# Transposes of the identity into an idle PSUM bank during the opening waits of a two-stream attention and expert kernel

## What is computed

```python
x = x + 0.5 * ffn(layernorm(x), ...)      # first half
x = x + attn(layernorm(x), ...)           # middle: grouped-query attention with rotary embedding
x = x + 0.5 * ffn(layernorm(x), ...)      # second half, same weights as the first
```

## Time and profile before

| What | Value |
|---|---|
| Median of 3 runs | 1806.88 us |
| Lowest, highest | 1806.15, 1808.86 us |
| The profiled execution | 1805.85 us |
| Its span, first to last instruction | 1803.9 us |
| TensorE matmuls busy | 1436.7 us (80%) |
| VectorE busy | 1197.7 us (66%) |
| ScalarE busy | 1095.6 us (61%) |
| GpSimd busy | 620.2 us (34%) |
| Mean granted TensorE clock | 0.913 of 2.4 GHz |

### The profile page before, as it was taken

The page is one execution under the profiler, slowest core; times in us unless marked ns, Lnnn a source line. Parts: engine busy times, 40 slices in busy tenths (PEclk is TensorE's granted clock), DMA queues, the critical chain, the costliest instruction groups (busy, mean ns, idle before and its releaser), DMA issues. The chain is left out here.

```text
span 1803.9 us, 34159 instructions
## 1 busy us (share of the span) xinstructions
PE 1436.7 (80%) x11800; PEld 640.8 (36%) x11801; DVE 1197.7 (66%) x1856; ACT 1095.6 (61%) x2032; POOL 620.2 (34%) x897
## 2 busy tenths in 40 slices
PE   2899999999508963799999999999999999607970
PEld 1333333433305541333333333333333433305540
DVE  5788888887202326588888888888888888112322
ACT  1578878878303321578888888887878887403320
POOL 1333343311261122646644433332333311261126
PEclk8799999999758985799999999999999999858995
DMA  6533444421011114333333333323333321011113
GB/s 207 128 91 104 106 112 118 126 64 31 1 47 46 47 33 101 73 87 102 86 95 77 84 99 90 85 71 94 81 96 81 94 50 31 1 45 45 44 32 92
DMA packets 85126, 139.57 MB, mean 77 GB/s; under 512 B 26736, under 2 KB 53104, under 8 KB 84976
## 3 DMA queue, kind: packets, MB, share of 16 engines
q1 hardware_dynamic: 57264, 83.24, 17.8%
q0 software_dynamic: 25664, 48.32, 10.8%
q10 hardware_dynamic: 2048, 6.03, 1.0%
HBM read 78.47 MB, written 56.10 MB: 75 GB/s over the span
## 5 line engine op out<-in xcount | busy, mean ns | idle before, releaser
L929 DVE TENSOR_REDUCE maxima<-banks 128x2 f32<-128x1024 f32 x768 | 925.0, 1223 | 174.1 <-PE banks L610 168.4
L906 ACT ACTIVATE work<-banks 128x512 f32<-128x512 f32 x1536 | 829.1, 598 | 121.6 <-PE banks L626 106.7
L610 PE MATMUL banks<-K,Q 64*128 64x512 f32 x1536 | 571.4, 461 | 67.4 <-DVE maxima L929 35.3
L626 PE MATMUL banks<-Q,K 64*128 64x512 f32 x1536 | 567.6, 451 | 9.1 <-ACT work L906 8.5
L638 PE MATMUL banks<-work,V 128*9 128x256 f32 x6144 | 476.6, 382 | 2.3 <-ACT work L906 0.8
L610 PEld LDWEIGHTS banks<-K,Q 64*128 64x128 f32 x1536 | 229.4, 189 | 225.4 <-DVE maxima L929 121.3
L626 PEld LDWEIGHTS banks<-Q,K 64*128 64x128 f32 x1536 | 229.1, 185 | 190.9 <-issue 140.8
L638 PEld LDWEIGHTS banks<-work,V 128*9 128x9 f32 x6144 | 91.5, 88 | 276.3 <-issue 205.8
L545 POOL TENSOR_TENSOR lo<-full,hi 128x512 fp32r<-128x512 f32 x44 | 56.2, 1277 | 312.6 <-ACT hi L813 214.0
L1295 ACT ACTIVATE work<-banks,ln 128x128 f32<-128x128 f32 x80 | 36.5, 457 | 187.1 <-PE banks L1244 187.1
L1319 DVE COPY work<-banks 128x512 f32<-128x512 f32 x80 | 55.3, 691 | 121.8 <-PE banks L1255 121.1
(11 more groups left out here) (153 smaller groups left out, 1373.6 us busy)
## 6 DMA issues: line engine op xcount, KB each, us to landing
Q<-q_scratch SPq DMA_DIRECT2D x188, 192.0 KB, 3.5
K<-k_scratch SPq DMA_DIRECT2D x376, 64.0 KB, 3.2
q_scratch<-hi POOLq DMA_DIRECT2D x44, 256.0 KB, 4.6
q_scratch<-lo POOLq DMA_DIRECT2D x44, 256.0 KB, 6.7
k_scratch<-hi POOLq DMA_DIRECT2D x22, 256.0 KB
k_scratch<-lo POOLq DMA_DIRECT2D x22, 256.0 KB
work<-sorted_x SPq DMA_DIRECT2D x80, 64.0 KB, 1.7
sorted_y<-work POOLq DMA_DIRECT2D x80, 64.0 KB, 1.8
```

Source lines behind the costliest of these rows:

```text
L610: fill(nc.tensor.matmul(bank, q4[parts(j), n % SLOTS, j // 2, qt * P:(qt + 1) * P], k4[parts(j), n % SLOTS, j // 2, :], start=True, stop=T ...
L626: nc.tensor.matmul(scp[x % EXPS][:, :], k4[parts(j), n % SLOTS, j // 2, kt * P:(kt + 1) * P], q4[parts(j), n % SLOTS, j // 2, :], start=Tr ...
L906: nc.scalar.activation(prob[:, kt, j ^ 1, :], scp[x % EXPS][:, :], ACT.Exp, scale=SCALE).then_inc(s.probs, 1)
L929: nc.vector.tensor_reduce(c.maxima[:, at:at + 9:8], c.banks[:, k * S:(k + 2) * S].rearrange("p (m n) -> p m n", m=2), AX.X, ALU.max).then_ ...
```

## The change

A list `WARM` gives three counts for each stream. A helper issues that many transposes of the identity matrix, with the identity as the other operand, into the first 128 columns of bank 4. None of them waits for a semaphore or signals one. They stand in three places of TensorE's program: before everything else of the stream (60 in stream 0, 90 in stream 1), before `loaded(0)` (100 and 150), and after the four matmuls of each query tile in the maxima of step 0 (10 each time, so 40 per stream). The tile's name in the trace is `banks<-ident`.

```diff
@@ -52,6 +52,7 @@
 AHEAD = 2
 SLOTS = 5
 EARLY = 2
+WARM = ((60, 100, 10), (90, 150, 10))
@@ -737,6 +738,11 @@
                 for j in range(J):
                     max_score(n, qt, j)
 
+            def warm_up(n):
+
+                for _ in range(n):
+                    nc.tensor.transpose(scp[0][:, 0:P], c.ident[:, :], c.ident[:, :])
+
@@ -757,14 +763,17 @@
+            warm_up(WARM[label][0])
             if label == 0:
                 pe.wait_ge(c.weights, 16 * c.first_loads)
             for n in range(-8, -4):
                 group(n, 0)
                 group(n, 2)
+            warm_up(WARM[label][1])
             loaded(0)
             for qt in range(QT):
                 maxima(0, qt)
+                warm_up(WARM[label][2])
             turn_max(0)
             loaded(1)
```

## The result

The changed kernel took 1815.36 us in the median of six runs (1813.72 to 1818.68), the kernel before 1806.88 in its six. The ratio is 1.0049 with an interval of 1.0036 to 1.0062, about 9 us slower, and outside the range. The profiled execution took 1818.68, the slowest of the six; its span is 1816.8 against 1803.9. So its own 12.8 us are not the median's 9.

What follows compares the result with a forecast made beforehand. It held that waits bound the openings, with slow-clock TensorE work on stream 1's path, and VectorE the maxima of step 0. Gains of 2.25 and 1.84 us summed to 4.1, from 1806.88 to 1802.8 us; range 1796 to 1808.

Steps and rivals of the forecast that it cites:

- 90 in stream 1: Train at stream 1's start: 12.4 us, from 669.6 to 682.0, hidden by a wait until 682.2.
- All slow, 19.8: Upper bound for the 90 transposes at stream 1's start if all ran at 1.2 GHz, ending at 689.4.
- rival 3: Both streams: transposes do not hold the clock up, all take 0.22 us; 29 to 39 us slower; chance 0.12.
- Transposes count for the clock: All trains: transposes count as work for TensorE's clock, so it rises; based on one mixed stretch with four transposes.
- 60: Train at stream 0's start: 9.1 us, from 6.9 to 16.0, hidden by VectorE's norm.
- 100: Train before stream 0's load: 11 us, from 25.5 to about 36.6, covered by the DMA wait until 38.1.
- 150: Train before stream 1's load: 16.5 us, from 690.7 to 707.2, against a wait until 708.0.
- Stream 1, first part, 2.25 us: Stream 1's opening: transposes 0.5 us sooner, projections q and qs 1.75 less, carried through to 708.0.
- The maxima, 0.92 per stream: From the first maxima into step 1's: faster matmuls and transposes save 0.92 us, twice 1.84.
- The tens, "cost nothing": After each query tile: 1.1 us fast, hidden under VectorE's 2.28; if slow, 2.3 us per stream.
- Maxima of step 1 stay slow: Rest of step 1's maxima, both streams: clock expected to fall after the last ten transposes, so no gain.
- rival 1: Clock lasts through step 1's maxima: some 4 us more in stream 0, about 2 in stream 1; 1797; chance 0.18.

Runs made afterwards that it cites:

- e5_gathers_late: Changed kernel with all trains, eight of the twelve gathers moved behind batch 0's norm in stream 1; ratio 0.9998 to the kernel before.
- e4_wide: Changed kernel with stream 1's 90 transposes replaced by 12 matmuls of 512 columns; ratio 1.0002 to the kernel before.
- e9_best: Kernel before plus trains of 90, 120 and 10 in stream 1 only, with eight gathers late; ratio 0.9995 to the kernel before.
- e13_wide_late: Kernel before plus 12 and 15 wide matmuls in stream 1 only, with eight gathers late; ratio 0.9984 to the kernel before.
- e12_tens: Kernel before plus only the 10 transposes after each query tile, in both streams; ratio 1.0027 to the kernel before.
- e11_hundred: Kernel before plus only the 100 transposes before the load in stream 0; ratio 1.0003 to the kernel before.
- e7_sixty: Changed kernel with 60 transposes instead of 90 at the start of stream 1; ratio 1.0037 to the kernel before.
- e8_wide_s1: Kernel before plus wide matmuls in stream 1 only (12, 17, 1), gathers not moved; ratio 1.0005 to the kernel before.
- e2_only90: Kernel before plus only the 90 transposes at the start of stream 1; ratio 1.0034 to the kernel before.
- e14_wide_all_late: Kernel before plus wide matmuls (0, 15, 1 in stream 0; 12, 15, 0 in stream 1), eight gathers late; ratio 0.9976 to the kernel before.
- e6_wide_all: Changed kernel with all trains as wide matmuls (8, 13, 1 and 12, 17, 1), gathers not moved; ratio 0.9989 to the kernel before.

## Why the prediction was wrong, point by point

- **The step that failed** is "90 in stream 1: 5 + 67 x 0.11 = 12.4 us, from 669.6 to 682.0, against 682.2". The train took 20.4 us there, to 692.1, and 12.2 in e5_gathers_late, where eight gathers come later. The price was right for a train with four gathers beside it. What failed with it is the sentence "Nothing queues behind a new wait, since none is added, and no DMA is issued", which put the cost of the neighbours at nothing. I had looked at the stretch for what TensorE waits for, not for what else was at work: twelve indirect DMAs on GpSimd. I named only the wait until 682.2 as cover and priced nothing for the neighbours. "All slow, 19.8" was in the list of bounds, and nearly what happened, but I gave it the cause of a cold clock and the chance of rival 3. What did happen, a train that overshoots although the clock is up, had 0.02.
- **Transposes count for the clock**: right. It reads 0.50 beside transposes alone from 671.7 to 677.6 and 1.00 behind them. The Trainium skill, "TensorE: Matmul & The Clock Gate", Part 4: PE-mode transpose, holds that the full clock does not engage in transpose mode; these rows disagree, and the measurement decides. So rival 3 had the sign, by luck, and not the mechanism: its pace of 0.22 all through did not occur, nor its 29 to 39 us. The working of the slow step is circular as written (0.43 from 0.22 and 0.22 from 0.43); the steps measured, 0.21 to 0.22 slow and 0.11 fast, bear it out.
- **60**: forecast 9.1 us and an end at 16.0; measured 9.21 from 6.94, an end at 16.15. Right.
- **100**: forecast 11, to 36.6; measured 11.34, to 36.5. Right. The first maximum was 0.8 late all the same, which I had put at nothing.
- **150**: forecast 16.5, measured 16.57. Right in size, but the cover was as thin as I wrote: with the stall gone the first maximum began right at its end (e4_wide, e5_gathers_late), so the gain before it could not pass. 120 and 15 wide ones leave the room.
- **Stream 1, first part, 2.25 us**: right in size where nothing stalls. From the first transpose to SyncE's first write of Q it is 2.3 to 2.4 in all four kernels with trains and late gathers (9.33 against 6.95 to 7.02). Up to the first maximum it is 2.0 in e9_best and 2.4 in e13_wide_late; in e5_gathers_late 0.8 (23.75 against 24.54), for its 150 end last. In the changed kernel the stall swallowed it.
- **The maxima, 0.92 per stream**: right in stream 1 of the changed kernel, where the first maximum and the end of the transposes in the maxima of step 1 lie 13.27 us apart (716.92, 730.19) against 14.20 before (707.99, 722.19). In stream 0 the cold tens ate it: 14.67 (38.90, 53.57) against 14.19.
- **The tens, "cost nothing"**: nearly right in stream 1 of the changed kernel, where ten take 1.31 us and the eight reductions fill 9.34 instead of 9.14. In stream 0 TensorE had waited 2.4 us, the clock had dropped, and the first ten starved VectorE by 1.11. The bound of 2.3 us per stream for cold ones was near (e12_tens, 1.5 and 1.9).
- **Maxima of step 1 stay slow**: right in stream 0, 0.50 from 53.0. In stream 1 the clock is up for part of them in both kernels, 0.83 in the changed one over 727.4 to 745.2 and 0.69 before over 718.5 to 736.3. The exit, ScalarE's copy of the high part behind the rotation, comes 32.90 us after the first maximum (716.92, 749.82) against 34.02 (707.99, 742.01), 1.1 less, which is the 0.92 and not the 2 on top of it that rival 1 had for this stream. Rival 1 falls.
- **The profiled 12.8 us**: 2.0 were there when stream 1 opened (GpSimd's first gather at 672.42 against 670.45) and 8.9 at its first maximum (716.92 against 707.99). The rest comes later, where this execution's clock reads 0.50 for 3.3 us near 793.7 and again near 913.2, and the one before reads 1.00 all through. The same happens in e11_hundred, with no train in stream 1 (0.99 over 760 to 1000), so I don't count it to the change, though no run shows that the change has no part in it. The median's 9 us are less than 12.8.

**What stays open** is what in the gathers holds up the other engines. The steps of 0.7 us set in after 72 or 73 transposes, whatever stands before them, and end as the last gather lands; ScalarE's wait fits no counter in the trace, and it does not end with the landing: GpSimd's own wait for the gathers is over at 689.06 in e7_sixty and at 688.64 in e8_wide_s1, and ScalarE's copy starts at 689.90 and 687.20. A fetch of instructions is the near guess: the Trainium skill, "Runtime: NRT & Kernel Launch", Instruction fetch mechanics, says that the sequencers are refilled in blocks of 16 KiB, mostly hidden. The trace has them as packets of 0.02 MB in a queue of their own, 95 in the changed kernel and 91 before. But the one near the stall comes at 681.0 in the changed kernel and at 670.6 in e2_only90, whose stall is the same, one at 679.0 does no harm in e5_gathers_late, and in e7_sixty there is none from 660 to 696, where ScalarE is 4.4 us late. The recorded packets don't settle it. It wasn't tried whether a train that follows the gathers' last landing, or gathers that carry fewer rows each, would be free of it.

## What to carry to other kernels

Filling an idle engine to keep its clock up is no free work, even when every instruction ends before the wait it hides in: look at what the neighbours do in that window (here indirect DMAs on GpSimd), and move them away from it. Few instructions, wide matmuls rather than transposes, helped beside them, but only in part. Let a train end some microseconds ahead of its cover, since the gain that it brings moves the cover forward too, and put none between tiles unless the clock is already up when it starts. The two pull against each other: after 2.4 us of waiting at the load the clock was at 0.50 here, after 0.7 (e14_wide_all_late) it was still up. Then test one train at a time, for the whole change showed only the loss of one of its trains.

## What the runs showed of the hardware that I had not expected

- 90 transposes beside twelve gathers: 73 at the full pace, then one every 0.7 or 1.4 us with the engine waiting for nothing the profile shows, until the last gather landed. The same 90 without eight of the gathers: 12.2 us.
- ScalarE began a copy 4.4 us late behind 60 transposes beside the gathers, and 1.6 to 3.3 late behind 12 wide matmuls (e4_wide, e8_wide_s1, e6_wide_all), with no slow step on TensorE. 30 transposes did nothing.
- fp32 transposes of the identity alone raise the clock to 2.4 GHz (0.50 until 677.6 and 1.00 from 677.7, six us into a train) and hold it there: 100 in 11.34 us, 150 in 16.57.
